# A DLRM tower on one core: layer 1 of the first tile in two half-width pieces, the dense part and layer 3 moved ahead of the dots, one more gather up front

## What is computed

```
combined = concat([dense[:, None, :], e], axis=1)        # (512, 27, 128)
inter = einsum('bnd,bmd->bnm', combined, combined)       # (512, 27, 27)
z = concat([dense, inter[:, upper triangle]], axis=1)    # (512, 479)
h = concat([z, dense], axis=1)                           # (512, 607)
h = relu(h @ W_top1 + b_top1)                            # (512, 512)
h = relu(h @ W_top2 + b_top2)                            # (512, 256)
y = h @ W_top3                                           # (512, 1)
```

## Time and profile before

| | |
|---|---|
| time, median of 3 runs (lowest, highest) | 122.82 us (122.56, 123.43) |
| time of the profiled execution | 122.21 us |
| its span, first to last instruction | 120.4 us |
| granted TensorE clock, mean | 1.000 of full speed |
| TensorE matmul busy | 105.6 us (88%) |
| weight loads busy | 91.8 us (76%) |
| VectorE, ScalarE, GpSimd busy | 85.6, 78.1, 56.6 us |

### The profile page before, as it was taken

The page is one execution under the profiler, slowest core; times in us unless marked ns, Lnnn a source line. Parts: engine busy times, 40 slices in busy tenths (PEclk is TensorE's granted clock), DMA queues, the critical chain, the costliest instruction groups (busy, mean ns, idle before and its releaser), DMA issues. The chain is left out here.

```text
span 120.4 us, 2635 instructions
## 1 busy us (share of the span) xinstructions
PE 105.6 (88%) x1036; PEld 91.8 (76%) x1036; DVE 85.6 (71%) x170; ACT 78.1 (65%) x146; POOL 56.6 (47%) x64
## 2 busy tenths in 40 slices
PE   0058999899999999999999996699599979999991
PEld 0045787788888888888888986698589968999990
DVE  5599979999999998989552799697136680476002
ACT  4087738999999898893943699579335480447020
POOL 3377777787877777787771000078003800000000
DMA  3899999995578978852120000001100100000000
GB/s 92 244 410 404 379 389 389 347 304 192 193 299 240 340 226 252 352 203 60 45 65 22 0 5 0 5 22 46 27 0 5 44 22 5 0 0 8 0 0 1
DMA packets 5582, 16.97 MB, mean 141 GB/s; under 512 B 1473, under 2 KB 1729, under 8 KB 5442
## 3 DMA queue, kind: packets, MB, share of 16 engines
q1 hardware_dynamic: 3890, 13.64, 31.5%
q0 software_dynamic: 1536, 3.15, 9.1%
q10 hardware_dynamic: 144, 0.02, 0.1%
HBM read 16.80 MB, written 0.00 MB: 140 GB/s over the span
## 5 line engine op out<-in xcount | busy, mean ns | idle before, releaser
L337 POOL DMA_INDIRECT rows<-tbl,ids_sb x48 | 53.5, 1114 | 16.8 <-issue 12.0
L509 DVE TENSOR_SCALAR onehot<-ids_row,row_number 128x1024 fp32r<-128x1024 int32 x49 | 33.6, 754 | 1.9 <-PE acc_ps L620 1.4
L355 DVE COPY z<-dots_ps 30x128 f32<-30x128 f32 (+5 forms) x80 | 21.0, 263 | 5.9 <-PE dots_ps L682 3.8
L378 ACT ACTIVATE z<-dots_ps 30x128 f32<-30x128 f32 (+5 forms) x80 | 19.7, 246 | 8.3 <-PE dots_ps L682 7.1
L610 PE MATMUL acc_ps<-onehot,table_hi 128*128 128x512 f32 x68 | 17.3, 407 | 7.7 <-ACT table_hi L378 7.7
L610 PEld LDWEIGHTS acc_ps<-onehot,table_hi 128*128 128x128 f32 x68 | 13.1, 196 | 10.8 <-issue 7.2
L378 ACT ACTIVATE table_hi<-table_raw 128x1024 fp32r<-128x1024 f32 (+1 forms) x16 | 15.1, 979 | 7.9 <-DMA table_raw<-picked_tables 7.9
L682 PE MATMUL dots_ps<-cols 128*64 128x52 f32 x512 | 16.4, 222 | 4.1 <-DVE z L355 2.0
L682 PEld LDWEIGHTS dots_ps<-cols 128*64 128x64 f32 x512 | 15.6, 138 | 5.3 <-issue 2.4
L522 DVE TENSOR_TENSOR table_lo<-table_raw,table_hi 128x1024 fp32r<-128x1024 f32 (+1 forms) x16 | 17.1, 1113 | 0.1
L620 PE MATMUL acc_ps<-onehot,table_lo 128*128 128x512 f32 x68 | 17.1, 404 | 0.0
(11 more groups left out here) (43 smaller groups left out, 76.3 us busy)
## 6 DMA issues: line engine op xcount, KB each, us to landing
table_raw<-picked_tables SPq DMA_DIRECT2D x14, 512.0 KB, 7.2
ids_row<-ids_picked SPq DMA_DIRECT2D x7, 512.0 KB, 4.6
table_raw<-w SPq DMA_DIRECT2D x1, 1536.0 KB, 9.7
rows<-tbl,ids_sb POOLq DMA_INDIRECT x48, 4.4
w_sb<-w SPq DMA_DIRECT2D x1, 512.0 KB, 10.6
table_raw<-picked_tables SPq DMA_DIRECT2D x2, 128.0 KB, 4.8
dense_sb<-dense SPq DMA_DIRECT2D x1, 256.0 KB, 9.7
ids_sb<-ids ACTq DMA_DIRECT2D x1, 24.0 KB, 3.7
```

Of the source, the lines that this page charges most:

```text
L337: nc.gpsimd.indirect_dma_start(rows[:, t % GATHER_RING, n, :], None, tables[GATHERED[n]][:, :], index).then_inc(rows_in[t][g], 16)
L355: last = copy(z[QUAD * q:QUAD * q + rows_of, t % 2, :, QUAD * s + b0:QUAD * s + b1], src.rearrange("i b c -> i c b"))
L378: return nc.scalar.activation(dst, src, ACT.Copy)
L509: nc.vector.tensor_scalar(onehot[:, c], ids_row[:, pair % IDS_RING], row_number[first_row][:, c:c + 1], None, ALU.is_equal).then_inc(oneho ...
```

## The change

Layer 1 of tile 0 no longer runs as one block of 16 matmuls after `dots(1)`. It is split into two pieces of 64 samples, 16 matmuls each with the same stationary weights and half the moving columns: piece 0 between the halves of `dots(1)`, piece 1 after `turn(2,2)`. `layer1_dense(1)` and `layer3(0)` come ahead of `dots(2)`; `layer3(1)` comes ahead of `dots(3)`, `layer1_dense(2)` between its halves. Layer 2 and `y` of tile 0 move to the banks of the turned groups, with the waits that this needs. The first pause comes one gather later, and `dots(0)` waits for 42 gathers in place of 41.

```diff
-LATE_GATHER = 41
+LATE_GATHER = 42
-PAUSES = {41: 1, 45: 2}
-LANDED = {0: 41, 2: 45}
+PAUSES = {42: 1, 45: 2}
+LANDED = {0: 42, 2: 45}
@@ h2_ps, y_ps
-            if t >= TILES - 2:
+            if t != 1:
                 return turn_ps[o][:, 0, :]
-            return turn_ps[1][0:1, 1, :] if t >= TILES - 2 else acc_ps[1][0:1, 2 * P:3 * P]
+            return turn_ps[0][0:1, 1, :] if t != 1 else acc_ps[1][0:1, 2 * P:3 * P]
@@ turn
+                if t == TILES - 1:
+                    pe.wait_ge(y_moved, 1)
@@ layer1_dense
                     if t >= 1 and o == 0:
                         pe.wait_ge(h1_ready["scalar"], t)
-                        pe.wait_ge(h2_ready["scalar"], min(t, TILES - 2))
+                    if t >= 2 and o == 0:
+                        pe.wait_ge(h2_ready["scalar"], 2)
                     if t >= 1 and o == H1_ACT:
                         pe.wait_ge(h1_ready["vector"], t)
-                        pe.wait_ge(y_moved, min(t, TILES - 2))
+                    if t >= 2 and o == H1_ACT:
+                        pe.wait_ge(y_moved, 2)
@@ new
+            def layer1_piece(i):
+                b0, b1 = PARTS[i]
+                def samples(columns):
+                    return columns.rearrange("p (s b) -> p s b", b=QUAD)[:, :, b0:b1]
+                pe.wait_ge(z_ready["scalar"], 2 * (i + 1))
+                pe.wait_ge(z_ready["vector"], 2 * (i + 1))
+                for o in range(K1):
+                    for c in range(CHUNKS):
+                        last = nc.tensor.matmul(samples(h1_ps(o)), w1_sb[:, c, o * P:(o + 1) * P],
+                                                samples(z[:, 0, c, :]), start=False, stop=(c == CHUNKS - 1),
+                                                skip_group_check=True)
+                    if i == 1 and o in (H1_ACT - 1, H1_ACT):
+                        last.then_inc(layer1_done, 1)
@@ layer2
                 if t == 0:
                     pe.wait_ge(w2_in, 16)
-                if t >= 1:
+                    for engine in ("scalar", "vector"):
+                        pe.wait_ge(turned_moved[engine], moved_count(engine, 2, len(GROUPS[2]) - 1))
+                if t >= 2:
                     pe.wait_ge(y_moved, t)
@@ layer3
-                pe.wait_ge(h2_ready["scalar"], t + 1)
-                pe.wait_ge(h2_ready["vector"], t + 1)
-                for k in range(K2):
+                if t == 1:
+                    pe.wait_ge(h2_ready["vector"], t + 1)
+                for k, engine in enumerate(("scalar", "vector")):
+                    pe.wait_ge(h2_ready[engine], t + 1)
@@ the order on TensorE after turn(2, 1)
+            dots(1, lambda: layer1_piece(0))
             turn(2, 2)
+            layer1_piece(1)
+            layer2(0)
+            layer1_dense(1)
+            layer3(0)
+            dots(2, between)                     # between: turn(3, 0), turn(3, 1)
+            layer1(1, range(H1_ACT))
+            layer1(1, (H1_ACT,))
+            layer2(1)
+            turn(3, 2)
+            turn(3, 3)
+            layer3(1)
+            dots(3, lambda: layer1_dense(2))
+            layer1(2, range(H1_ACT))
+            layer1(2, (H1_ACT,))
+            layer2(2)
+            layer1_dense(3)
+            layer3(2)
+            layer1(3, range(H1_ACT))
+            layer1(3, (H1_ACT,))
+            layer2(3)
+            layer3(3)
```

More of the change, by code:

```diff
@@ L746, in _, with between @@
             turn(2, 1)
-            dots(1)
+            dots(1, lambda: layer1_piece(0))
             turn(2, 2)
[L749 to L767, removed]
+            layer1_piece(1)
+            layer2(0)
+            layer1_dense(1)
+            layer3(0)
+            def between():
+                turn(3, 0)
+                turn(3, 1)
+            dots(2, between)
[15 more added lines that the diff above has]
+            layer3(3)
 def kernel(**inputs):
```

## The result

The changed kernel's comparable executions take 1.0123 times those of before (95% interval 1.0073 to 1.0173), with the kernel before at 122.78 us: about 124.3 us, or 1.5 us more. The median of all its six is 125.41 us, because three of them ran at a mean clock of 0.986 and 2 us longer than the other three; the ratio leaves those three out. The profiled execution took 124.41 us with a span of 122.6 us, 2.2 us more than before.

What follows compares the result with a forecast made beforehand. TensorE, 88% busy, was taken as the bound. Gather +0.4, overfilled hole +1.9, work moved into the wait ahead of dots(2) -1.6 and +0.2 later make +0.9 us: 123.1 profiled, 123.7 as median, range 121.8 to 124.6.

Steps and rivals of the forecast that it cites:

- The sum of +0.9 us: Whole kernel: all terms on TensorE together, from 122.21 to 123.1 us in the profiled execution, 123.7 us as median.
- The likeliest outcome: Whole kernel: a time within 1% of the kernel before, chance 0.66.
- the hoisted steps: Layer 1's dense part and layer 3 moved into the wait ahead of dots(2): -1.6 us, then +0.2 net further on.
- The pieces: Half-width layer 1 of tile 0: 3.6 us each, 7.2 us for both in place of 3.57.
- weight load against moving side: Pace of layer 1's half-width matmuls: weight load keeps 0.112 us a record; moving columns would give 0.058.
- Overfilled hole: Between the halves of dots(1): piece 0 with switches takes 3.8 us and outlasts the 1.78 us hole, +1.9 us.
- The moving-bound rival: Layer 1 of tile 0: moving columns set the pace, 1.9 us a piece, time 122.0; chance 0.24 in all.
- The 42nd gather: Start of dots(0): the added gather starts at 64.10 and lands at 66.56, dots(0) at 66.65, +0.4 us.
- the rival with dots(0) at 67.7: Start of dots(0): added gather is long or starts behind long ones; total +1.9 us, 124.7; chance 0.10.
- Ahead of dots(2): Start of dots(2): at 88.25 in place of 86.0, +2.25 us.
- The cover: Ahead of dots(2): gathers land at 86.7, while TensorE's own work runs to 88.25 and hides that wait.
- Stages 3 and 4: After dots(2): turn(3,3) waits 0.5 us for its gather, dots(3) +1.35, layer 1 of tile 2 +0.9 us.

Runs made afterwards that it cites:

- the two comparisons: The unaltered changed kernel measured twice against the kernel before: ratio 1.0123 first, then 1.0062 when run again on another chip.
- e4: Kernel before with only the 42nd gather put ahead of the pause and waited for: ratio 1.0014 to the kernel before.
- e2: Changed kernel with layer 1 of tile 0 whole, 42 gathers and moved steps kept: ratio 0.9947 to the kernel before.
- e3: Changed kernel with layer 1 of tile 0 whole and 41 gathers, leaving only the moved steps: ratio 0.9905 to the kernel before.
- the second group: Follow-up runs made together on another chip, beside runs of the kernel before, which took 126.1 us there.
- e5: Changed kernel with layer 1 whole, 41 gathers, layer3(1) back between the halves of dots(3), layer1_dense(2) behind them: ratio 0.9891 to the kernel before.

## Why the prediction was right

It was right in sign and in the main mechanism. The sum of +0.9 us was somewhat small, with about +1.5 by the ratio, 124.3 us against 123.7; the profiled spans are 2.2 apart, the one of before being one of the shortest. The likeliest outcome (0.66) was a time within 1% of before; 1.2% lies just past it, and the two comparisons (1.0123 and 1.0062) do not tell on which side of 1% the kernel is. That the forecast came this close is in part luck. Between the profiled executions two terms were too favourable, the gather by 1.1 us and the hoisted steps by 0.5, and one of 0.3 us that was put at nothing went the other way.

- **The pieces.** The step that decided the sum, weight load against moving side, held: 0.112 us a record forecast, 3.72 us for 32 with the switch measured, and 0.112 with 32 moving columns too. Overfilled hole: 1.9 forecast; from the first to the second half of dots(1) it was 3.86 us before and 5.72 after. With the load formula of the Trainium skill ("TensorE: Matmul & The Clock Gate", section "LDWEIGHTS (loading the stationary operand)") the trace agrees: an estimated 107 ns for a load of 128 columns by the page, 112 ns of pace in the pieces. The moving-bound rival is refuted for this shape.
- **The 42nd gather.** The term that was mis-sized most: +0.4 forecast, +1.53 measured in that execution, +0.84 in e4; in e2 dots(0) did not wait for it at all. By the ratios it is 0.5 to 0.8 us. It was to start at 64.10 and started at 64.97, since the 41 gathers in front of it took 48.26 us on GpSimd, 1.47 more than before, though they began 0.57 earlier; and from its start to TensorE's first record went 2.81 us, where I had 2.55 from one later gather. This is the place of the rival with dots(0) at 67.7; it came true (67.78) in the profiled execution, through the sum of several longer gathers, which its words "or starts behind such" cover, and not through the 42nd being a long one. It had a chance of 0.10.
- **Ahead of dots(2).** Forecast +2.25; measured +3.51, which is 2.38 without the 1.13 us too little at dots(0). The cover held: TensorE's own work releases dots(2).
- **Stages 3 and 4.** turn(3,3) waits 0.57 us for its gather (0.5 forecast). Layer 1 of tile 2 was 2.40 us late; the forecast is 2.03 with the gather's real price put in. The rest is 0.13 us at dots(2) and 0.2 from layer 1 of tile 1 to dots(3). The last gathers were let go 2.98 us later, 1.85 without the gather's 1.13; I had 1.65, where my own figures (2.25 less 0.53) give 1.72. Behind that, layer 1 of tile 2 takes 0.10 us more directly behind dots than behind the dense part.
- **What I did not cost.** layer3 now waits for ScalarE's half of h2 alone before its first matmul. At the tail this gives 0.3 us back, in e3 as here: from the start of layer 2 to the end of the last copy it was 3.41 us before (115.41 to 118.82) and is 3.10 after (117.91 to 121.01). I had put it at nothing.
- **The hoisted steps.** I had -1.6 us, with 0.2 lost again further on: -1.4. By the trace of e3 they are worth 0.86 us. The 1.52 forecast up to layer 1 of tile 1 came out in the changed kernel (3.51 us late at dots(2), 1.99 at layer 1), but 0.84 us was lost again up to dots(3), where the gathers set the time, for 0.65 forecast; 0.13 more went at dots(2) and 0.10 at layer 1 of tile 2. The pieces and the gather together cost more than the hoist gave.

## What to carry over

A split that halves only the moving columns of float32 matmuls with 128 stationary ones saves no TensorE time where load and multiply are balanced: every piece pays for all the weights again. Before filling a hole, compare its length (1.8 us) with the work put in (3.7 us), and ask whether the work is taken away elsewhere; moving whole existing steps into waits gave 0.9 us here, while the split layer, which loads its weights twice, lost 1.9. A producer that runs back to back from the start shows its slack only for the one execution that was traced. Work added to it should be priced with the spread of all its items, not with the length of the common one. And a change that carries several edits can hold one that nobody priced: the split wait of layer3 gave 0.3 us.

## What the runs showed of the hardware

Gathers of one kernel and one table list don't take the same time in every run. The 42nd of them started at 64.97 us in the changed kernel, at 64.11 in e4 and at 63.31 in e2. Single gathers take mostly 0.94 to 1.07 us, but several in each run take 1.1 to 1.5 us or 1.97, and the same one can be long in one run and short in another, here the 33rd in the changed kernel and in e2:

```profile
52.09 1.97 POOL L337 DMA_INDIRECT rows<-tbl,ids_sb  x1 [0.30 <-issue]
```

```profile
50.70 1.02 POOL L337 DMA_INDIRECT rows<-tbl,ids_sb  x1 [0.30 <-issue]
```

The first 41 take 46.79 us together before and 48.26 in the changed kernel. What makes them long stayed open.

On the chip of the second group VectorE resumed late after waits that the trace marks as remote, in e5 ahead of activate1(0), and TensorE had a hole of 0.97 us in the middle of layer 2, at the matmul that waits for this row, that the first chip never showed:

```profile
86.05 0.29 DVE L558 TENSOR_SCALAR h<-acc_ps 128x128 f32<-128x128 f32 x1 [2.25 <-remote]
```

```profile
86.40 1.38 PE L746 MATMUL turn_ps<-h,w_sb 128*128 128x128 f32 x10 [0.97 <-issue]
```

The kernel before took 3.3 us more there (126.1 against 122.8). The cause was not tried.
